# The end of the attention stage: the maximum over partitions behind the first head's power, the last outputs scaled in three parts, the first tile's chain ahead of the second's

## The chip, the core and the metric

The kernel runs on one NeuronCore of a Trainium2 chip. A core has TensorE (PE), VectorE (DVE), ScalarE (ACT), GpSimd (POOL) and SyncE (SP), which here issues nearly all transfers; each runs its own instruction stream and waits for the others on semaphores. The metric is the time of one execution on the device, in microseconds (us), lower is better.

## The reference

A pre-norm decoder layer with three parts over `x` of 16 batches, 256 positions, 512 channels:

```python
x = x + _L0_attn_ref(_layernorm(x, axis=-1), L0_attn_w_qkv, L0_attn_w_proj)
x = x + _L0_xattn_ref(_layernorm(x, axis=-1), L0_xattn_k, fside_S2_0, ctx_2048, ctx_2048, 8)
x = x + _L0_ffn_ref(_layernorm(x, axis=-1), L0_ffn_gate_w, L0_ffn_up_w, L0_ffn_down_w, ...)

def _bitlinear(x, w):        # attention's two linear layers
    xq = round_and_clip(x * 127 / max|x| over the row) / that factor
    wq = round_and_clip(w / mean|w|, -1, 1) * mean|w|
    return xq @ wq.T
# attention: 16 heads of 32 channels, causal softmax, then _bitlinear with w_proj
# mixer: kv = v (x) x2 of each pair of 8 channels, long convolution with k, + kv * skip, times x1, summed
# feed-forward: silu(x @ fp8(gate_w) * gate_scale) * (x @ fp8(up_w) * up_scale), @ fp8(down_w) * down_scale
```

(The lines of `_bitlinear` and the comments are condensed.) The place of the change is the seam between the first part, whose last batch must be scaled, rounded, multiplied and added to `x`, and the second, whose heads need rows of every batch.

## The kernel before

Every engine's stream is written out by hand as a Python function that walks the same step counter, so the order on an engine is the order of the code.

**Attention** goes through `B * PAIRS` = 128 pairs of heads (16 batches, 8 pairs each), one new pair per step. For pair n: `row_max` and `take_max` find the rows' maxima (bank `s_qk`); `probabilities` (PE) writes the scores into bank `s_kq`; `exponentials` (ACT) makes `pT`; `high_part` copies it to `pH` (f16; ACT, the first pair of a batch DVE); `low_part` (POOL) makes the rest `pL`; `weigh` (PE) multiplies both with the values into bank `pv`; `weighed` (ACT) copies `pv` into `oraw`. There is one `s_kq` and one `pv`: the scores of pair n wait for the exponentials of n-1, and `weigh` for the copy before it.

**A batch's end.** `oraw` has for each of two position tiles t and each head 32 outputs in two halves (high and low part of v) and the denominator. The halves are added (tile 0 DVE, tile 1 POOL, `sum_parts`), divided by the denominator (L1063 for the last batch), their largest magnitude is taken (L1066), ACT makes the step of it (L1486), DVE the inverse (L1070, L1074), ACT rounds (L1488), PE turns the tile (`turn_oq`), ACT copies it as `oqT` (L1475), PE multiplies with the weights (`project_out`, L684) and DVE adds the product to `x` (`add_out`, L1045). For the last batch, 15, `finish_last` does this once all 128 pairs are through; batch 14's last steps are mixed in.

**The next part.** SP brings rows of batches 14 and 15 from `x_sb` into `x_grp` as soon as tile 0 of the batch has been added. Head 0 is then prepared (`prepare(0, k)`): DVE takes the moments (L1182 to L1187), POOL raises to the power -1/2 (L1845) and multiplies (L1847), ACT normalises (`v_sb`, L1608), PE turns, ACT copies (`vT`, L1623), and `kv` = `vT` times `cT` in four blocks of 1024 columns: blocks 0 and 1 on DVE (L1194), blocks 2 and 3 on POOL (L1866). `mix` on PE (L803) goes through rows 0, 2, 1, 3 of blocks, two halves each; row 0 needs block 0, row 2 needs blocks 0, 1 and 2. A matmul of f32 shows as two records.

**The maximum over partitions.** The feed-forward part needs a bound of its weights' sizes. `mx` is ready at 425.4 us; POOL's `partition_all_reduce` (L1837) takes the maximum over partitions into `mall`, and DVE makes the scales of it in seven small instructions (`fuse_bound`, L1288 to L1301).
Of the kernel before, what the change touches and what calls it, by code (L numbers as in the profile page):

```python
# [14 lines left out]
P = 128  # L15
# [52 lines left out]
def decoder_kernel(nc, x, skip, ctx_in, w_qkv, w_proj, k_turned, w_gate, w_up, w_down,  # L68
# [21 lines left out]
    HIGH_ON_ACT = (1, 2, 3, 4, 5, 6, 7)  # L90

    with ExitStack() as ctx:
# [164 lines left out]
        high_act, high_dve, low_done = signal("p_high_act"), signal("p_high_dve"), signal("p_low")  # L257
# [36 lines left out]
        PREFETCH_AT, PREFETCHED_AT = B * PAIRS - 2, B * PAIRS + PROB  # L294
# [54 lines left out]
        WEIGHT_BOUND_AT, REDUCE_AT = (PIECES - 1) * PAIRS + CLAMP_AT + 1, (B - 1) * PAIRS + FINISH + 1  # L349
# [6 lines left out]

        def high_done(n):
            b, p = divmod(n, PAIRS)
            if p in HIGH_ON_ACT:
                return high_act, b * len(HIGH_ON_ACT) + HIGH_ON_ACT.index(p) + 1  # L360
            other = [i for i in range(PAIRS) if i not in HIGH_ON_ACT]
            return high_dve, b * len(other) + other.index(p) + 1
# [109 lines left out]
        SCALE_DOWN_AT = 20  # L472
# [73 lines left out]
        def tensor_program(tensor):  # L546
# [83 lines left out]
            def probabilities(n):  # L630
# [4 lines left out]
                def scores(to, h, key, query, first):  # L635
                    r, g = h % R, h // R
                    T.matmul(to, pack[:, 1, r, g, key * P:(key + 1) * P], pack[:, 0, r, g, query * P:(query + 1) * P],  # L637
                             start=first, stop=False)

                w.wait_ge(exp_done, n)  # L640
                T.matmul(s_kq[:, 0:4, :], ident_b[:], mask_kq[:], start=True, stop=False)
                w.wait_ge(mT_low, use + 1)
                for hh in range(2):
                    h = 2 * p + hh
                    for tile in range(2):
                        scores(s_kq[:, 2 * hh + tile, :], h, tile, tile, False)
                    T.matmul(s_kq[:, 2 * hh:2 * hh + 2, :], pick[:, h % H_HEADS, :], nt[:, 0:N], start=False, stop=hh == 1)
                for hh in range(2):
                    h = 2 * p + hh
                    scores(s_kq[:, 4 + hh, :], h, 0, 1, hh == 0)  # L650
                    made = T.matmul(s_kq[:, 4 + hh, :], pick[:, h % H_HEADS, :], nt[:, P:N], start=False, stop=hh == 1)  # L651
                made.then_inc(st_pe, 1)

            def weigh(n):
# [4 lines left out]
                w.wait_ge(low_done, n + 1)  # L659
# [51 lines left out]
            for t in STEPS:  # L711
# [6 lines left out]
                for b, k in batches(t, FINISH, 14):  # L718
# [10 lines left out]
                    elif k == 0:  # L729
                        turn_oq(b, 0)  # L730
# [22 lines left out]
                if t == PREFETCHED_AT:  # L753
                    turn_c(0, misc1)
# [134 lines left out]
        def vector_program(vector):  # L889
# [122 lines left out]

            def finish(b, k):
# [34 lines left out]
            def finish_last():  # L1048
# [9 lines left out]
                w.wait_ge(oqT_pe, 2 * b)
                w.wait_ge(ostep_done, b - 1)
                for t in range(NT):  # L1060
                    if t == 1:
                        w.wait_ge(o_sum, B)
                    V.tensor_tensor(o_sb[:, t, 0:C].rearrange("p (h d) -> p h d", d=D), raw[:, t, :, 0:D],  # L1063
                                    rl[:, t, :].unsqueeze(2).broadcast_to([P, HEADS, D]), ALU.mult).then_inc(o_mult, 1)
                    w.wait_ge(o_mult, b + t + 1)
                    V.tensor_reduce(out=am[:, t:t + 1], in_=o_sb[:, t, :], op=ALU.max, axis=AXIS.X,  # L1066
# [1141 lines left out]
```

## Time and profile before

| | us |
|---|---|
| three timed runs | 1482.04, 1484.29, 1485.83 (median 1484.29) |
| profiled execution | 1481.37 |
| its span, first to last instruction | 1479.6 |
| attention, to the last pair's `oraw` | 0 to 462.2 |
| seam, to the first `mix` matmul | 462.2 to 481.6 |
| mixer and feed-forward | 481.6 to 1479.6 |

PE is busy for 1391.8 us (94%), DVE 1233.3 (83%), POOL 1178.9 (80%), ACT 871.6 (59%). These shares are means over parts with different limits; for a change in the seam only the chain of waits there and what follows on PE count.

### The profile page before, as it was taken

How to read it: one execution, taken by the hardware profiler on the slowest of the kernel's cores; microseconds unless marked ns; L12 is line 12 of the kernel's file. 1: busy time of each engine (PE TensorE's matmuls, PEld its weight loads, DVE VectorE, ACT ScalarE, POOL GpSimd, SP SyncE). 2: the span in 40 equal slices, each digit the busy share in tenths (PEclk: the TensorE clock that was granted, in tenths of full speed). 3: DMA queues.
4: the chain of work that ended last, by engine and by line, in shares of the span. 5: the costliest groups of instructions: out<-in, count | busy, mean ns of one | idle time of the engine just before them, and what ended most of it. 6: DMA issues, size and time to landing. Idle time of an engine off the chain costs nothing.

```text
span 1479.6 us, 23950 instructions
## 1 busy us (share of the span) xinstructions
PE 1391.8 (94%) x8405; PEld 773.0 (52%) x8405; DVE 1233.3 (83%) x1964; ACT 871.6 (59%) x1437; POOL 1178.9 (80%) x902
## 2 busy tenths in 40 slices
PE   3788999999986997999999999999999999999998
PEld 2677878787863442334444444444444444444443
DVE  6889999999884898899898899899889889888511
ACT  5689999999885123544455545464455446544341
POOL 3389999999985787888888888878887888888532
PEclk9899999999997999999999999999999999999999
DMA  5654646464622533222513421432323232240001
GB/s 193 155 126 117 171 133 172 136 171 122 158 67 75 173 79 88 55 57 64 107 44 72 89 61 43 93 78 50 79 65 77 62 76 57 65 100 15 21 15 29
DMA packets 171587, 133.57 MB, mean 90 GB/s; under 512 B 120500, under 2 KB 124748, under 8 KB 171468
## 3 DMA queue, kind: packets, MB, share of 16 engines
q1 hardware_dynamic: 171276, 131.91, 35.6%
q8 instruction: 67, 1.10, 0.3%
q14 instruction: 52, 0.43, 0.1%
q10 hardware_dynamic: 192, 0.14, 0.1%
HBM read 50.67 MB, written 19.92 MB: 48 GB/s over the span
## 4 chain that ended last, share of the span: by engine, by line
PE 65%; DVE 11%; POOL 8%; issue 7%; ACT 6%; DMA 1%; SPq 0%; POOLq 0%; DVEq 0%; ACTq 0%
PE gu L844 20%; PE gu L858 11%; PE shared_bank L789 9%; POOL pL L1796 3%; PE y L811 3%; PE y L808 3%; PE y L805 3%; PE y L813 3%; PE y L814 3%; DVE blockmax L987 2%; DVE o_sb L1027 2%; PE gu L803 1%; PE y L803 1%; DVE qkt L967 1%; ACT pH L1439 1%
## 5 line engine op out<-in xcount | busy, mean ns | idle before, releaser
L1668 ACT ACTIVATE shared<-shared_bank 128x512 f32<-128x512 f32 x162 | 96.2, 594 | 322.9 <-PE shared_bank L789 322.9
L1219 DVE TENSOR_TENSOR y<-shared,y 128x512 f32<-128x512 f32 x324 | 224.1, 692 | 42.7 <-ACT shared L1668 23.0
L1796 POOL TENSOR_TENSOR pL<-pT,pH 128x768 f16<-128x768 f32 x128 | 216.8, 1696 | 13.6 <-ACT pH L1439 7.7
L1226 DVE TENSOR_REDUCE oT<-z 128x64 f32<-128x512 f32 x256 | 175.6, 686 | 8.7
L844 PE MATMUL gu<-fT,wg 128*128 128x512 f16 x768 | 181.4, 379 | 1.5 <-DMA fT<-fnl 1.5
L844 PE MATMUL gu<-fT,wu 128*128 128x512 f16 x768 | 182.5, 381 | 0.0
L1222 DVE TENSOR_TENSOR z<-y,cT 128x512 f32<-128x512 f32 x236 | 162.4, 688 | 11.0 <-PE y L803 4.4
L1930 POOL TENSOR_TENSOR fuL<-fu,fuH 128x512 f16<-128x512 f32 x96 | 112.0, 1166 | 71.7 <-ACT fuH L1683 71.5
L858 PE MATMUL gu<-wd,fuH 128*128 128x512 f16 x384 | 145.5, 379 | 0.0
L858 PE MATMUL gu<-wd,fuL 128*128 128x512 f16 x384 | 145.5, 379 | 0.0
L1866 POOL TENSOR_TENSOR kv<-vT,cT 128x1024 f32<-128x1024 f32 x70 | 137.8, 1970 | 6.1 <-ACT vT L1623 6.1
L844 PEld LDWEIGHTS gu<-fT,wg 128*128 128x128 f16 x768 | 75.0, 98 | 120.5 <-issue 47.4
L844 PEld LDWEIGHTS gu<-fT,wu 128*128 128x128 f16 x768 | 75.5, 98 | 119.5 <-issue 47.2
L1433 ACT ACTIVATE pT<-s_kq,ws 128x768 f32<-128x768 f32 x128 | 115.0, 898 | 26.9 <-PE s_kq L651 20.2
L987 DVE TENSOR_REDUCE blockmax<-s_qk 128x6 f32<-128x768 f32 x124 | 117.6, 948 | 3.9 <-PE s_qk L621 2.7
L789 PE MATMUL shared_bank<-kv_sum,toep 128*128 128x512 f32 x216 | 111.2, 597 | 0.3 <-POOL kv_sum L1854 0.3
L1854 POOL TENSOR_TENSOR kv_sum<-kv 128x1024 f32<-128x1024 f32 x27 | 63.7, 2360 | 55.2 <-DVE kv L1194 55.2
L637 PE MATMUL s_kq<-pack 128*128 128x128 f16 x768 | 99.4, 220 | 0.0
L1241 DVE SCALAR_TENSOR_TENSOR fu<-gu,cols,sil 128x512 f32<-128x512 f32 x96 | 71.4, 743 | 33.6 <-PE gu L844 33.6
L1789 POOL TENSOR_TENSOR qkhl<-qkt,qkhl 128x512 f16<-128x512 f32 x62 | 83.9, 1354 | 19.2 <-ACT qkhl L1419 19.2
L1439 ACT ACTIVATE pH<-pT 128x768 f16<-128x768 f32 x112 | 94.0, 840 | 0.0
L1194 DVE TENSOR_TENSOR kv<-vT,cT 128x1024 f32<-128x1024 f32 x58 | 75.1, 1297 | 14.2 <-ACT vT L1631 11.5
(231 smaller groups left out, 3561.8 us busy)
## 6 DMA issues: line engine op xcount, KB each, us to landing
pack<-qkhl SPq DMA_DIRECT2D x256, 128.0 KB, 2.6
x_sb<-in_x SPq DMA_DIRECT2D x16, 512.0 KB, 4.0
c_sb<-in_ctx SPq DMA_DIRECT2D x32, 256.0 KB, 4.0
hankel<-in_L_xattn_k SPq DMA_DIRECT2D x32, 256.0 KB, 4.1
out_y<-yo SPq DMA_DIRECT2D x32, 256.0 KB, 2.9
x_grp<-x_scratch SPq DMA_DIRECT2D x30, 256.0 KB, 3.5
x_scratch<-x_sb SPq DMA_DIRECT2D x14, 512.0 KB, 3.0
wraw<-in_L_attn_w_qkv SPq DMA_DIRECT2D x3, 1024.0 KB, 9.6
```

Of the source, the lines that this page charges most:

```text
L789: T.matmul(shared_bank[:], tap(h, (2, 0, 1)[part]), (kv_sum, kv12, kv_sum)[part][:, half * HB:(half + 1) * HB, :, :].rearrange("p b j i -> ...
L844: made = T.matmul(bank[:], (wg, wu)[which][:, cb, ib * P:(ib + 1) * P], fT[:, cb, part, :], start=cb == 0 and part == 0, stop=cb == CB - 1 ...
L858: made = T.matmul(bank[:], src[:, t * P:(t + 1) * P], wd[:, ib, :], start=ib == 0 and part == 0, stop=ib == IB - 1 and part == 1)
L987: V.tensor_reduce(out=blockmax[b % 2][:, p, :], in_=score_tile(n)[:, 0:6, :], op=ALU.max, axis=AXIS.X, negate=True).then_inc(max_done, 1)
L1219: chain.step(V.tensor_tensor(bank[:], shared[2 * part + half][:], bank[:], op))
L1222: V.tensor_tensor(z[:], y, weight, ALU.mult).then_inc(m_zm, 1)
L1226: V.tensor_reduce(out=oT[h % 2][:, lb, own].rearrange("p (b j) -> p b j", b=HB), in_=z[:], op=ALU.add, axis=AXIS.X).then_inc(m_z, 1)
L1433: S.activation(pT[n % NP][:], s_kq[:, 0:6, :], ACT.Exp, scale=ws[:, 4:5]).then_inc(exp_done, 1)
L1439: S.activation(pH[n % NP][:], pT[n % NP][:], ACT.Copy).then_inc(high_act, 1)
L1796: G.tensor_tensor(pL[n % 2][:], pT[n % NP][:], pH[n % NP][:], ALU.subtract).then_inc(low_done, 1)
L1866: G.tensor_tensor(block(h, lb), vT[:, lb, :].rearrange("p (b i) -> p b i", b=B).unsqueeze(2).broadcast_to([P, B, M_POS, M_POS]), cT[h % 2] ...
L1930: G.tensor_tensor(fuL[ib][:], fu[n % 2][:], fuH[:, ib, :], ALU.subtract).then_inc(f_fl, 1)
```

## The change

It does six things, all at attention's end.

1. The scores of odd pairs of the last batch go into `s_qk`, which is free once all maxima are taken, so that two score banks take turns.
2. The last pair's `pH` and `pL` are made by DVE (`low_part` on DVE), no longer by ACT and POOL.
3. `toep` and `cT` of head 0 (two ACT copies), and the turning of `c_sb` on PE ahead of `cT`, move from step 136 into the last batch's finish: `toep` between tile 0's rounding and its `oqT` copy, `cT` behind that copy.
4. Tile 0 of the last batch is scaled in three parts, after pairs 4, 7 and 8 of the batch; the first part's halves are added by POOL (`sum_first`). The result lies in `xn`. The maxima of the parts are joined by one more instruction. The step is made by DVE, not ACT.
5. ACT's order becomes tile 0 to its `oqT` copy, then tile 1. On DVE `add_out(14, 0)` moves behind tile 1's scaling.
6. The all-reduce moves on POOL behind the power and product of head 0, in front of its `kv` blocks; `fuse_bound` moves on DVE from the preparation of head 0 to step 8 of the mixer.

The order on POOL, at the change of part, before:

```order
L1796 TENSOR_TENSOR pL1<-pT1,pH1 128x768 [waits pv_pe,p_high_act]
L1801 TENSOR_TENSOR oraw1<-oraw1 128x16x32 [waits pv_out]
L1837 ISA
L1837 ISA mall<-mx 128x4 [waits mx]
L1845 ISA
L1845 TENSOR_TENSOR mstat0<-mstat0,minus_half 128x1 [waits packed2,packed0,v_pe,s_pe,qk_low,st_pe,qk_scaled,m_var,cbc_pe,xqT_pe]
L1847 TENSOR_TENSOR mstat0<-mstat0 128x1 [waits m_rstd]
L1866 TENSOR_TENSOR kv0<-vT,cT0 128x1024 [waits m_vT,m_cT]
```

and on the same engine at the same place after the change:

```order
L1844 TENSOR_TENSOR oraw1<-oraw1 128x8x32 [waits pv_out]
L1849 TENSOR_TENSOR oraw1<-oraw1 128x16x32 [waits pv_out]
L1892 TENSOR_TENSOR mstat0<-mstat0,minus_half 128x1 [waits packed2,packed0,v_pe,s_pe,qk_low,st_pe,qk_scaled,m_var,cbc_pe,xqT_pe]
L1894 TENSOR_TENSOR mstat0<-mstat0 128x1 [waits m_rstd]
L1897 ISA
L1897 ISA mall<-mx 128x4 [waits mx]
L1916 ISA
L1916 TENSOR_TENSOR kv0<-vT,cT0 128x1024 [waits m_vT,m_cT]
```

The last pair's `pL` is gone, half of tile 0's sum is new, and the all-reduce with its two switches stands between the product and `kv` block 2 in place of between the sum and the power.

DVE in the last batch's finish, before:

```order
L1055 RECIPROCAL osmall1<-oraw1 128x32 [waits pv_out]
L1056 TENSOR_TENSOR oraw1<-oraw1 128x16x32
L1063 TENSOR_TENSOR o_sb<-oraw1,osmall1 128x512 [waits oqT_pe,vec_step]
L1066 TENSOR_REDUCE osmall1<-o_sb 128x1 [waits o_mult]
L1070 RECIPROCAL osmall1<-osmall1 128x1 [waits ostep]
L1045 SCALAR_TENSOR_TENSOR x_sb6<-misc2,osmall0,x_sb6 128x512 [waits proj_pe,c2]
L1063 TENSOR_TENSOR o_sb<-oraw1,osmall1 128x512 [waits o_sum]
L1066 TENSOR_REDUCE osmall1<-o_sb 128x1 [waits o_mult]
L1074 RECIPROCAL osmall1<-osmall1 128x1 [waits ostep]
```

and after, from tile 0's third part on:

```order
L1093 RECIPROCAL osmall1<-oraw1 128x2 [waits pv_out]
L1097 TENSOR_TENSOR oraw1<-oraw1 128x2x32
L1081 TENSOR_TENSOR xn<-oraw1,osmall1 128x64 [waits vec_step]
L1107 TENSOR_REDUCE osmall1<-xn 128x1 [waits o_mult]
L1110 TENSOR_SCALAR osmall1<-osmall1 128x1 [waits vec_step]
L1086 TENSOR_SCALAR osmall1<-osmall1 128x1 [waits vec_step]
L1088 RECIPROCAL osmall1<-osmall1 128x1 [waits ostep]
L1112 RECIPROCAL osmall1<-oraw1 128x16
L1081 TENSOR_TENSOR xn<-oraw1,osmall1 128x512 [waits o_sum,vec_step]
L1117 TENSOR_REDUCE osmall1<-xn 128x1 [waits o_mult]
L1086 TENSOR_SCALAR osmall1<-osmall1 128x1 [waits vec_step]
L1088 RECIPROCAL osmall1<-osmall1 128x1 [waits ostep]
```

Behind the last of these rows stands now `add_out(14, 0)`, which stood between the tiles (`x_sb6<-misc2`); behind the last pair only 64 columns of tile 0 are left.

The diff, cut to its core:

```diff
@@ numbers of the plan
-    HIGH_ON_ACT = (1, 2, 3, 4, 5, 6, 7)
+    HIGH_ON_ACT, LAST_HIGH_ON_ACT = (1, 2, 3, 4, 5, 6, 7), (1, 2, 3, 4, 5, 6)
+        LAST_AT = B * PAIRS - 1 + LOW
+        LAST_PARTS = ((0, PAIRS // 2), (PAIRS // 2, PAIRS - 1), (PAIRS - 1, PAIRS))
+        LOW_ON_DVE = [B * PAIRS - 1]
+        def scores_tile(n):
+            return s_qk if n > (B - 1) * PAIRS and n % 2 == 1 else s_kq
@@ PE, probabilities
-                w.wait_ge(exp_done, n)
+                if n > (B - 1) * PAIRS:
+                    w.wait_ge(exp_done, n - 1)
+                    w.wait_ge(max_done, B * PAIRS)
+                else:
+                    w.wait_ge(exp_done, n)
+                to = scores_tile(n)
@@ PE, the last batch
                     elif k == 0:
+                        turn_c(0, misc1)
                         turn_oq(b, 0)
                         project_out(b, 0)
                         project_out(b - 1, 1)
@@ DVE, finish_last
+                for i, (begin, stop) in enumerate(LAST_PARTS):
+                    first, end = 2 * begin, 2 * stop
+                    w.wait_ge(pv_out, PAIRS * b + stop)
+                    chain.step(V.reciprocal(rl[:, 0, first:end], raw[:, 0, first:end, D]))
+                    if i == 0:
+                        w.wait_ge(o_sum, B)
+                    else:
+                        chain.step(V.tensor_tensor(raw[:, 0, first:end, 0:D], raw[:, 0, first:end, 0:D], raw[:, 0, first:end, VW:VW + D], ALU.add))
...
+                step_last(0)
+                chain.step(V.reciprocal(rl[:, 1, :], raw[:, 1, :, D]))
                 chain.wait()
...
+                w.wait_ge(o_sum, B + 1)
+                scale_heads(1, 0, HEADS).then_inc(o_mult, 1)
...
+                step_last(1)
+                w.wait_ge(c2_done, b)
+                add_out(b - 1, 0)
                 w.wait_ge(c2_done, b + 1)
                 add_out(b, 0)
                 add_out(b - 1, 1)
@@ DVE, mixer
-                if k == 1:
-                    fuse_bound()
+                if g == FUSE_BOUND_AT:
+                    fuse_bound()
@@ ACT, finish_last
                 for t in range(NT):
-                    w.wait_ge(omax_done, b + t + 1)
-                    S.activation(step[:, t:t + 1], am[:, t:t + 1], ACT.Copy, scale=1.0 / 127.0).then_inc(ostep_done, 1)
                     w.wait_ge(oscale_done, b + t + 1)
-                    S.activation(o_sb[:, t, 0:C], o_sb[:, t, 0:C], ACT.Copy, bias=ROUND, scale=inv[:, t:t + 1]).then_inc(o_round, 1)
+                    S.activation(xn[:, t, 0:C], xn[:, t, 0:C], ACT.Copy, bias=ROUND, scale=inv[:, t:t + 1]).then_inc(o_round, 1)
...
+                        projected(w)
+                        turn_taps(0)
+                    copy_oqT(b, t)
+                    if t == 0:
+                        copy_cT(0, misc1)
@@ POOL
+            def sum_first():
+                raw, heads = oraw[(B - 1) % 2], slice(0, 2 * LAST_PARTS[0][1])
...
-                if t == REDUCE_AT:
-                    w.wait_ge(mx_done, 1)
-                    G.partition_all_reduce(mall[:], mx[:], P, RMAX).then_inc(mall_done, 1)
@@ POOL, prepare
                     G.tensor_tensor(shift, shift, rstd, ALU.mult).then_inc(m_shift, 1)
+                    if h == 0:
+                        w.wait_ge(mx_done, 1)
+                        G.partition_all_reduce(mall[:], mx[:], P, RMAX).then_inc(mall_done, 1)
```

## Rows read from the trace of the kernel before

**Rows 1.** Chain of waits through the seam: start us, us, what.

```profile
461.85 0.40 ACT oraw L1447
...
468.97 0.59 ACT oqT L1475
...
469.69 1.88 PE misc L684 x4
...
472.44 1.96 DMA x_grp<-x_sb
...
475.76 0.71 issue
...
481.58 3.75 PE y L803 x4
```

**Rows 2.** ACT in order of time: start us, us, instruction [idle before <-releaser].

```profile
456.37 0.62 ACT L1505 ACTIVATE toep<-hankel 128x512 f32<-128x512 f32 x1
...
457.48 0.38 ACT L1447 ACTIVATE oraw<-pv 128x260 f32<-128x260 f32 x1
457.75 0.84 ACT L1439 ACTIVATE pH<-pT 128x768 f16<-128x768 f32 x1
...
465.92 0.72 ACT L1488 ACTIVATE o_sb<-o_sb,osmall 128x512 f32<-128x512 f32 x1 [0.23 <-DVE osmall L1070]
```

**Rows 3.** DVE in order of time, through the seam and head 1.

```profile
438.59 0.55 DVE L1011 CAST pH<-pT 128x768 f16<-128x768 f32 x1
...
464.69 0.69 DVE L1066 TENSOR_REDUCE osmall<-o_sb 128x1 f32<-128x513 f32 x1
...
476.48 0.18 DVE L1288 TENSOR_TENSOR bound<-mall 128x2 f32<-128x2 f32 x1
...
477.66 0.23 DVE L1301 TENSOR_SCALAR cols<-cols,bound 128x12 f32<-128x12 f32 x1
...
502.69 0.69 DVE L1222 TENSOR_TENSOR z<-y,cT 128x512 f32<-128x512 f32 x1 [2.02 <-PE y L803]
...
505.02 0.14 DVE L1187 TENSOR_SCALAR mstat<-mstat 128x1 f32<-128x1 f32 x1
```

**Rows 4.** POOL in order of time, from the last pair to head 2's power.

```profile
458.68 1.64 POOL L1796 TENSOR_TENSOR pL<-pT,pH 128x768 f16<-128x768 f32 x1 [0.58 <-ACT pH L1439]
462.31 1.06 POOL L1801 TENSOR_TENSOR oraw<-oraw 128x512 f32<-128x512 f32 x1 [2.00 <-ACT oraw L1447]
469.17 0.39 POOL L1837 PARTITION_ALL_REDUCE mall<-mx  x1 [5.79 <-issue]
476.47 0.59 POOL L1845 TENSOR_TENSOR mstat<-mstat,minus_half 128x1 f32<-128x1 f32 x1 [6.92 <-DVE mstat L1187]
...
480.25 2.99 POOL L1866 TENSOR_TENSOR kv<-vT,cT 128x1024 f32<-128x1024 f32 x1 [2.92 <-ACT vT L1623]
...
486.34 1.95 POOL L1866 TENSOR_TENSOR kv<-vT,cT 128x1024 f32<-128x1024 f32 x1
...
505.25 0.75 POOL L1845 TENSOR_TENSOR mstat<-mstat,minus_half 128x1 f32<-128x1 f32 x1 [2.75 <-DVE mstat L1187]
```

**Rows 5.** By line: POOL's library switches, xcount, duration ns, first and last start us.

```profile
L1742 POOLq MODIFY_POOL_CONFIG  x2: 11/11/11, 1.3 to 1.4; - x2
...
L1837 POOLq MODIFY_POOL_CONFIG  x2: 11/11/11, 463.3 to 463.4; - x2
...
L1845 POOLq MODIFY_POOL_CONFIG  x2: 82/82/83, 469.5 to 469.5; - x2
```

**Rows 6.** Windows: us, busy of PE, PEld, DVE, ACT, POOL; PEclk; DMA share; GB/s.

```profile
449.70:453.00 3.30, 3.10 (x35) 2.39 (x31) 2.46 (x1) 2.33 (x4) 3.30 (x3) 0.50 0.00 0
...
466.80:473.50 6.70, 4.82 (x15) 2.29 (x16) 2.15 (x5) 1.62 (x5) 0.39 (x1) 0.50 0.03 5
...
481.60:487.10 5.50, 5.50 (x7) 2.40 (x8) 5.29 (x8) 0.70 (x2) 3.10 (x4) 0.50 1.03 337
487.30:502.40 15.10, 15.10 (x42) 7.05 (x41) 9.14 (x15) 2.14 (x3) 11.67 (x8) 1.00 0.59 175
```

More of the change, by code:

```diff
@@ L355, in decoder_kernel, with high_on_act, low_parted @@
         wq8 = wq8_dram.rearrange("m n p c -> m (n p c)").rearrange("m (n p c) -> m n p c", p=P, c=PIECE)
+        def high_on_act(n):
+            return n % PAIRS in (HIGH_ON_ACT if n < (B - 1) * PAIRS else LAST_HIGH_ON_ACT)
         def high_done(n):
[L358 to L362, printed above, removed]
+            by_act = high_on_act(n)
+            return high_act if by_act else high_dve, sum(high_on_act(m) == by_act for m in range(n + 1))
+        def low_parted(n):
+            if n in LOW_ON_DVE:
+                return low_last, LOW_ON_DVE.index(n) + 1
+            return low_done, n + 1 - sum(m < n for m in LOW_ON_DVE)
+        def scores_tile(n):
+            return s_qk if n > (B - 1) * PAIRS and n % 2 == 1 else s_kq
         W_ORDER = (1, 0, 2, 3)
@@ L471, in row_of @@
             return SHARED_ROWS[s // 2]
-        SCALE_DOWN_AT = 20
+        FUSE_BOUND_AT, SCALE_DOWN_AT = 8, 20
         def groups(g, begin, steps):
@@ L1053, in finish_last @@
                 rl = osmall[:, 4 * NT:4 * NT + NT * HEADS].rearrange("p (t h) -> p t h", t=NT)
-                w.wait_ge(pv_out, PAIRS * B)
-                chain.step(V.reciprocal(rl, raw[:, :, :, D]))
-                chain.step(V.tensor_tensor(raw[:, 0, :, 0:D], raw[:, 0, :, 0:D], raw[:, 0, :, VW:VW + D], ALU.add))
-                chain.wait()
[L1058 to L1066, printed above, removed]
-                                    apply_absolute_value=True).then_inc(omax_done, 1)
-                    if t == 0:
-                        w.wait_ge(ostep_done, b + 1)
-                        V.reciprocal(inv[:, 0:1], step[:, 0:1]).then_inc(oscale_done, 1)
-                        w.wait_ge(c2_done, b)
-                        add_out(b - 1, 0)
@@ L1073, in finish_last, with scale_heads @@
-                w.wait_ge(ostep_done, b + 2)
-                V.reciprocal(inv[:, 1:2], step[:, 1:2]).then_inc(oscale_done, 1)
+                w.wait_ge(xqT_pe, 2 * B)
+                w.wait_ge(c2_done, b - 1)
+                chain.step(V.tensor_scalar(xn[:, :, C], ones[:, 0:NT], ws[:, 1:2], EPS, ALU.mult, ALU.mult))
+                def scale_heads(t, first, end):
+                    return V.tensor_tensor(xn[:, t, first * D:end * D].rearrange("p (h d) -> p h d", d=D), raw[:, t, first:end, 0:D],
+                                           rl[:, t, first:end].unsqueeze(2).broadcast_to([P, end - first, D]), ALU.mult)
@@ new lines, in finish_last @@
+                step_last(0)
+                chain.step(V.reciprocal(rl[:, 1, :], raw[:, 1, :, D]))
+                chain.wait()
+                w.wait_ge(o_sum, B + 1)
+                scale_heads(1, 0, HEADS).then_inc(o_mult, 1)
+                w.wait_ge(o_mult, b + 2)
+                chain.step(V.tensor_reduce(out=am[:, 1:2], in_=xn[:, 1, :], op=ALU.max, axis=AXIS.X, apply_absolute_value=True))
+                step_last(1)
+                w.wait_ge(c2_done, b)
+                add_out(b - 1, 0)
@@ L1141, in vector_program @@
                         low_max(use)
-                if (n := pair(t, HIGH)) is not None and n % PAIRS not in HIGH_ON_ACT:
+                if (n := pair(t, LOW)) in LOW_ON_DVE:
+                    low_part(n)
+                if (n := pair(t, HIGH)) is not None and not high_on_act(n):
                     high_part(n)
@@ L1552, in scalar_program @@
                     copy_weights(i, blocks)
-                if (n := pair(t, HIGH)) is not None and n % PAIRS in HIGH_ON_ACT:
+                if (n := pair(t, HIGH)) is not None and high_on_act(n):
                     high_part(n)
@@ L1820, in gpsimd_program @@
             for t in STEPS:
-                if (n := pair(t, LOW)) is not None:
+                if (n := pair(t, LOW)) is not None and n not in LOW_ON_DVE:
                     low_part(n)
+                if t == LAST_AT:
+                    sum_first()
                 for b, k in batches(t, FINISH, 1):
```

70 lines of the change are left out of this document (42 added, 28 removed).

## The prediction

> **What bounds the kernel now.** I read the chain of waits first, then each engine in order of time through the seam, then windows around it. The chain shows that from the last `oraw` copy (461.85) to the first `mix` matmul (481.58) one thing waits for another: 19.7 us in which no engine is full [rows 1]. From 481.58 on PE runs without a pause: 5.50 busy of 5.50, then 15.10 of 15.10 [rows 6]. So a microsecond taken out of the seam moves the whole mixer forward, unless PE runs into something that did not move with it. The reader is to see two other things. After the all-reduce POOL is not simply free [rows 4, 5]. And the granted clock after a pause of PE is 0.50 (1.2 GHz) for a while, 1.00 (2.4 GHz) again later [rows 6].
>
> **The change part by part.** All times are on the axis of the profiled execution (1481.37 us, span 1479.6, so 1.8 lie around it); it is 2.9 under the median of the runs, 1484.29.
>
> *The last `oraw` (parts 1 to 3).* In ACT's queue `toep` and `cT` stand from 456.37 to 457.48, 1.11 us, and behind them the copy that `weigh` of the next pair waits for; the last pair's `pH` costs up to 0.84 more there [rows 2]. POOL's last `pL` runs from 458.68 to 460.32 [rows 4]; on DVE the trace shows no such subtraction. Its bound from below is the 0.55 of the cast of 768 columns, from above POOL's 1.64 [rows 3, 4]; I take 0.96, since 512 columns cost 0.69 [rows 3], and DVE is idle there. Removing the 1.11 is certain; of the 0.84 a part is met by the turns through `pv` that remain; together I take 1.5 (1.1 to 1.95): the last copy starts at 460.35 in place of 461.85. The second score bank saves nothing by itself, since the exponentials there wait for POOL's `pL`, which the bank doesn't touch.
>
> *Tile 0 in three parts (4).* Before, the rounding starts at 465.92, 3.67 after the last copy's end (462.25) [rows 1, 2]. After the change seven small instructions follow the last copy; six starts of such take 1.18, from 476.48 to 477.66 [rows 3], so about 1.4. But DVE comes to them late: `pL` of the last pair until 458.8, then part one (two instructions of 256 columns, 0.42 each by the same line through 512 columns and the small ones) and part two (three of 192, 0.36 each), with gaps and reciprocals to 461.5. So the rounding starts at 463.1, 2.8 earlier.
>
> *Order of the tiles (5).* Before, tile 0's `oqT` copy (468.97) stands behind tile 1's rounding on ACT, 2.3 after the end of its own (466.64), and the multiplication starts at 469.69 [rows 1, 2]. After the change PE turns at 463.8 and ACT copies at 465.0. What is late next is `add_out(14, 0)`: it frees the bank that `project_out(15, 0)` takes, and now stands behind tile 1's whole chain on DVE: 0.25, 0.69, 0.69 [rows 3], two small ones, then 0.75, which end at 465.85. So the multiplication starts at 465.95: 3.7 earlier. The DMA of the rows (issued at 472.44, 1.96 us) [rows 1] and the moments shift by the same.
>
> *POOL's power.* In head 2 it starts 0.09 after DVE's release (505.16 to 505.25); in the seam the chain has 0.71 of issue between the release (475.76) and the power (476.47) [rows 1, 3, 4]. With the all-reduce no longer ahead some 0.7 go. The product then ends at 472.9 in place of 477.33, and `vT`, `kv` block 0 and the first `mix` matmul follow 4.4 earlier: 477.1 in place of 481.58.
>
> *The all-reduce's new place (6).* From the end of POOL's sum (463.37) to the start of the power (476.47) the all-reduce holds, or may hold, 13.1 us: 5.80 from the switch (463.4) to the all-reduce, 0.39 for it, and 6.91 from its end (469.56) to the power [rows 4, 5]. The first two are certain. Of the last 6.91 the wait for DVE covers 6.20; that the power came 0.7 later than it should says that POOL wasn't ready when DVE was. I read it as code loaded after a switch: 5.8 one way and up to 6.9 back. Its bounds are 0.7 (only a slow first call) and 6.91. I take 6.91, since the first switch took nearly as long without any wait, and since a shorter load back would have let the power start at the release. The switches at 1.3 cost nothing visible [rows 5], which speaks for the lower end; but there the standard code may have been in place already.
>
> Now this hides behind tile 1's chain and the DMA. After the change it stands in front of `kv` block 2: 472.9 + 13.1 = 486.0, and with 1.95 for the block [rows 4] it is ready at 487.95. PE needs it for the third product of row 2, after eight records. At the low clock these take 6.9 us (the seventh was under way when 5.50 were over) [rows 6]: PE stands from 484.0 to 488.0. Before, it reached the same product at about 487.8, the eighth record going at the high clock, with the block ready at 483.24 [rows 4, 6]. So the whole 4.4 us go back in one wait, and 0.2 more.
>
> The Trainium skill (GPSIMD Engine Reference, Instruction dispatch) says that the first call to a freshly loaded kernel pays about 6 us of code loading, 5.95 measured after MODIFY_POOL_CONFIG, with no instruction shown. This trace agrees for the all-reduce, 5.79 [rows 4]. For the way back, with the page's figure in place of 6.91, the block would be ready 1.0 earlier; read as paid by the call itself, whenever it comes, it would have put the power at 481.7, which the trace excludes.
>
> *The clock.* Before, PE is at 1.00 from 487.1 on. After a wait of 4 us it should come back low, as after its other pauses: low for 3.3 us from 449.7 and for 6.7 us from 466.8 [rows 6]. Half of that is lost, 1.65 to 3.35; I take 2.2 (0 if the pause is not noticed).
>
> *`fuse_bound`.* Seven instructions, 1.4 us from 476.48 to 477.9 [rows 3], free today because DVE waits there. Step 8 puts them into head 1 behind the 2.02 us in which DVE waits for PE [rows 3], so they don't fill that gap; there the banks ahead of PE may or may not take them up. 0 to 1.4, I take 0.6. The later `kv` blocks, `kv_skip` and head 1's power on POOL start 2 to 3 us later against PE, within gaps that POOL has in heads 0 and 1 (it is busy for 11.67 of 15.10) [rows 6]: nothing.
>
> Sum: -4.4 + 4.6 + 2.2 + 0.6 = +3.0 on the profiled execution, and the same on the median: 1487.3, rounded to 1487.
>
> **The rivals.**
> *A. Return without a load.* POOL is free 0.7 after the all-reduce. Then block 2 is ready at 472.9 + 5.8 + 0.4 + 0.7 + 1.95 = 481.8, before PE wants it at 484.0. For it: the free switches at the program's start; against it: the late power. Time: 1484.3 - 4.4 + 0.6 = 1480.5 (1478.5 to 1482.5).
> *B. The loads get slower: a loss.* Until 473.5 the DMA share was 0.03; from 481.6 it is 1.03 at 337 GB/s [rows 6], since SP then brings the feed-forward weights. The loads now fall into that. If code comes through the same memory and the 12.7 us become longer by a third to a half, PE waits another 4 to 6 us: 1491 to 1494, at 1492. It decides from a stretch of 12% on, where the total passes the bound below. For it: transfers there take longer; against it: no queue in the profile carries these loads.
> *C. The chain isn't shortened.* DVE's three parts collide with POOL's sum, or the last copy moves less: 2 us of the 4.4 are missing, block 2 comes later by as much: 1489.5.
>
> **How the numbers follow.** A run of this kernel can tell about 0.3%, 4.45 us, from no change: faster is under 1479.8, slower over 1488.7. Forecast (POOL held, PE waits): 0.62, of which 0.50 within the bound, 0.11 slower, 0.01 faster. A: 0.20, with 0.08 faster, 0.12 within. B: 0.12, slower 0.11. C: 0.06, slower 0.03. That gives faster 0.09, same 0.66, slower 0.25. The forecast's own range is 1484 to 1490.5. The range of all reaches down into A and up to the edge of B: 1480 to 1491.5; it leaves out the third of A with the largest gain and most of B, less than 2 in 10.
>
> **What would show it.** Right: the first `mix` matmul 4 to 5 us earlier against the last `oraw` of before (about 477), the power 0.1 after DVE's release, MODIFY_POOL_CONFIG right behind head 0's product, the all-reduce 5.8 later, `kv` block 2 about 13 us after the product, and PE idle for about 4 us in row 2 with POOL's `kv` as releaser, then a low clock. A is right if block 2 starts within 7.5 us of the product and PE shows no wait. B is right if the all-reduce starts over 7 us after its switch. I am wrong in the first part if `project_out(15, 0)` does not start near 466, and in the size if the clock stays at 1.00 after the wait.

## The result, and the profile after

The changed kernel takes **1490.0 us** (median of 5 runs, 1487.8 to 1492.2), the kernel before 1485.8 beside it (5 runs, 1482.0 to 1486.1): the ratio is 1.0035, 95% interval 1.0023 to 1.0048. The forecast was 1487.0. The profiled execution of after has a span of 1488.4 us, 8.8 more than that of before. Of these, 2.0 lie ahead of everything that the change touches: on POOL, `pL` starts at 419.07 us where it started at 417.08, and at 438.65 instead of 436.66, both ahead of the first pair whose scores are in another bank. Times of after in the seam are therefore compared with before's plus 2.0.

POOL of after in order of time (start us, us, instruction [idle before <-releaser]), beside [rows 4]:

```profile
475.88 0.56 POOL L1892 TENSOR_TENSOR mstat<-mstat,minus_half 128x1 f32<-128x1 f32 x1 [11.30 <-DVE mstat L1235]
476.52 0.19 POOL L1894 TENSOR_TENSOR mstat<-mstat 128x1 f32<-128x1 f32 x1
483.74 0.39 POOL L1897 PARTITION_ALL_REDUCE mall<-mx  x1 [7.03 <-issue]
491.62 1.94 POOL L1916 TENSOR_TENSOR kv<-vT,cT 128x1024 f32<-128x1024 f32 x1 [7.49 <-issue]
```

The library switches of after, by line (xcount, ns, first and last start us), beside [rows 5]:

```profile
L1897 POOLq MODIFY_POOL_CONFIG  x2: 11/11/11, 476.7 to 476.7; - x2
```
```profile
L1916 POOLq MODIFY_POOL_CONFIG  x2: 83/83/83, 484.1 to 484.1; - x2
```

PE of after in order of time, where row 2 stands still:

```profile
480.50 3.75 PE L820 MATMUL y<-kv,toep 128*128 128x512 f32 x4 [2.11 <-DVE kv L1242]
484.04 3.20 PE L820 MATMUL gu<-kv,toep 128*128 128x512 f32 x4
493.62 2.07 PE L820 MATMUL gu<-kv,toep 128*128 128x512 f32 x2 [6.38 <-POOL kv L1916]
```

Windows of after: us, busy of PE, PEld, DVE, ACT, POOL; PEclk (the clock granted to TensorE, 0.50 being 1.2 GHz); DMA share; GB/s, beside [rows 6]:

```profile
487.30:493.60 6.30, 0.00 (x0) 0.00 (x0) 0.00 (x0) 0.00 (x0) 1.98 (x2) 0.72 0.37 105
493.60:497.20 3.60, 3.58 (x8) 2.05 (x9) 1.44 (x3) 1.41 (x2) 3.39 (x4) 0.54 0.02 5
497.20:512.00 14.80, 14.80 (x39) 6.72 (x38) 9.36 (x14) 2.17 (x3) 10.03 (x7) 1.00 0.65 170
```

The reader is to see a core in which nothing computes for 4 us. The switch stands right behind POOL's multiplication with head 0's power (L1894); from 476.71 to 491.62, **14.9 us**, POOL executes one instruction of 0.39. Block 2 of `kv` waited for nothing else: its `vT` was there at 479.03. PE has done the two products that it can, waits 6.38 us for the block, and comes back at 1.2 GHz for 3.6 us. The front of the seam did get shorter: the first `mix` matmul starts at 480.50, against 481.58 + 2.0 [rows 1], 3.1 earlier. The third product of row 2, the first that needs block 2, starts at 493.62 against 487.88 + 2.0, 3.7 later, and head 1's products at 509.95 instead of 502.49, 5.5 later after the same correction.

### The profile page after: what moved, and what is told of

The parts are those of the page before. It is cut to its first block, busy times and chain, and to the rows that moved or that the text cites. A ratio compares the mean times of both kernels' runs of the same rounds, so it can differ in the third digit from the quotient of the medians.

```text
span 1488.4 us, 23963 instructions
## 1 busy us (share of the span) xinstructions
PE 1394.3 (94%) x8405; PEld 774.1 (52%) x8405; DVE 1235.1 (83%) x1978; ACT 870.5 (58%) x1434; POOL 1178.2 (79%) x902
## 4 chain that ended last, share of the span: by engine, by line
PE 63%; DVE 12%; POOL 8%; issue 8%; ACT 6%; DMA 2%; SPq 1%; POOLq 0%; DVEq 0%; ACTq 0%
PE gu L861 20%; PE gu L875 10%; PE shared_bank L806 9%; PE y L830 3%; PE y L831 3%; PE y L822 3%; PE y L825 3%; PE y L828 3%; POOL pL L1839 3%; DVE blockmax L1004 2%; DVE o_sb L1049 2%; DVE z L1270 1%; PE misc L702 1%; DVE qkt L984 1%; DVE osmall L1055 1%
## 5 line engine op out<-in xcount | busy, mean ns | idle before, releaser
L1839 POOL TENSOR_TENSOR pL<-pT,pH 128x768 f16<-128x768 f32 x127 | 215.7, 1701 | 15.4 <-PE pv L687 6.3
L1481 ACT ACTIVATE pT<-s_kq,ws 128x768 f32<-128x768 f32 x124 | 111.3, 898 | 26.4 <-PE s_kq L669 19.8
L1242 DVE TENSOR_TENSOR kv<-vT,cT 128x1024 f32<-128x1024 f32 x58 | 73.2, 1263 | 15.8 <-ACT vT L1674 12.7
```

The costliest lines, as they stand in the source:

```text
L1481: S.activation(pT[n % NP][:], scores_tile(n)[:, 0:6, :], ACT.Exp, scale=ws[:, 4:5]).then_inc(exp_done, 1)
L1839: G.tensor_tensor(pL[n % 2][:], pT[n % NP][:], pH[n % NP][:], ALU.subtract).then_inc(low_done, 1)
```

## The experiments

The times of before ran on the same chip as each experiment; ratios are to it.

**1. The all-reduce moved, alone.** Before, with part 6 of the change only:

```diff
-                if t == REDUCE_AT:
-                    w.wait_ge(mx_done, 1)
-                    G.partition_all_reduce(mall[:], mx[:], P, RMAX).then_inc(mall_done, 1)
...
                     G.tensor_tensor(shift, shift, rstd, ALU.mult).then_inc(m_shift, 1)
+                    if h == 0:
+                        w.wait_ge(mx_done, 1)
+                        G.partition_all_reduce(mall[:], mx[:], P, RMAX).then_inc(mall_done, 1)
```

> The kernel before with the sixth edit alone: the all-reduce behind head 0's product on POOL, fuse_bound at step 8. Theory (code loads hold POOL ahead of kv block 2, and PE waits there): the product ends some 0.7 us earlier, block 2 is ready about 17 us behind it, PE waits 5 to 6 us in row 2 and comes back at the low clock; together 6 to 9 us slower than before. Rival (the loss of the changed kernel comes from the rearranged finish, parts 1 to 5, and the all-reduce is harmless): within 1.5 us of before.

Measured: 1494.64 us, ratio **1.0069** (1.0050 to 1.0087). PE of this run:

```profile
480.52 3.75 PE L803 MATMUL y<-kv,toep 128*128 128x512 f32 x4 [2.11 <-DVE kv L1194]
484.06 1.98 PE L803 MATMUL gu<-kv,toep 128*128 128x512 f32 x4
492.86 2.07 PE L803 MATMUL gu<-kv,toep 128*128 128x512 f32 x2 [6.82 <-POOL kv L1866]
```

The loss is in this part, and it is larger without the rest of the change. It is also larger than was expected: 10.2 us by the ratio, where 6 to 9 stood, with a wait of PE of 6.82 where 5 to 6 stood; the way back took 7.85 here.

**2. Everything but that.** After, with the all-reduce and `fuse_bound` at their old places.

> The changed kernel with the sixth edit undone: all-reduce behind the last sum on POOL, fuse_bound in head 0's preparation. Theory (the way back to the standard code costs about 7 us whenever POOL has nothing to wait for, and now shows since the power is wanted earlier): the power starts 13 to 13.5 us after the sum's end and not when DVE releases it; 1 to 2 us faster than before. Rival (the way back is free and the 0.7 us were a slow first call): the power starts under 1 us after DVE's release, 2.5 to 3 us faster than before.

Measured: 1482.19 us, ratio **0.9989** (0.9980 to 0.9999). POOL of this run in order of time:

```profile
463.46 1.10 POOL L1849 TENSOR_TENSOR oraw<-oraw 128x512 f32<-128x512 f32 x1 [2.42 <-ACT oraw L1495]
470.82 0.39 POOL L1887 PARTITION_ALL_REDUCE mall<-mx  x1 [6.26 <-issue]
478.69 0.59 POOL L1895 TENSOR_TENSOR mstat<-mstat,minus_half 128x1 f32<-128x1 f32 x1 [7.47 <-issue]
```

DVE had released the power at 475.29 (its last small instruction: 475.15 and 0.14 long). The power starts 3.4 us after that, with no wait on record: the way back is bare here, 7.5 us from the all-reduce's end. Before, it was covered by the wait for DVE [rows 4]. So the place behind the last sum had just enough room for the old finish, and it holds up the new one; that is what the change ran away from, to a place with less room.

**3 and 4. No maximum over partitions.** After and before without the all-reduce: the bound is made from each partition's own maxima, so this step of the computation is missing in both.

```diff
-                w.wait_ge(mall_done, 1)
-                chain.step(V.tensor_tensor(bound[:], mall[:, 0:2], mall[:, 2:4], ALU.mult))
+                w.wait_ge(mx_done, 1)
+                chain.step(V.tensor_tensor(bound[:], mx[:, 0:2], mx[:, 2:4], ALU.mult))
...
-                        G.partition_all_reduce(mall[:], mx[:], P, RMAX).then_inc(mall_done, 1)
```

> The changed kernel without the all-reduce; the bound is taken from each partition's own maxima, so the maximum over partitions is left out. Theory: no wait of PE in row 2, high clock through it; 8 us faster than the changed kernel, about 3 to 4 us faster than before (0.2 to 0.3%). Rival (the finish costs as much as it gains): not faster than before.

> The kernel before without the all-reduce (bound from each partition's own maxima). Theory: the power starts 0.1 us after DVE's release, everything else as before: 0.7 us faster, no more. Rival (the all-reduce costs more there than the 0.7 us seen): over 1.5 us faster.

Measured: after without it 1479.84, ratio **0.9971** (0.9960 to 0.9982); before without it 1483.26, ratio **0.9998** (0.9989 to 1.0008). POOL and PE of the first of the two:

```profile
479.04 2.99 POOL L1913 TENSOR_TENSOR kv<-vT,cT 128x1024 f32<-128x1024 f32 x1 [2.46 <-ACT vT L1666]
```
```profile
480.37 3.36 PE L820 MATMUL y<-kv,toep 128*128 128x512 f32 x4 [2.11 <-DVE kv L1242]
483.56 2.74 PE L820 MATMUL gu<-kv,toep 128*128 128x512 f32 x6
```

One instruction of 0.39 us and its two switches cost nothing that can be measured in before's place on before's finish, 0.18% on the new finish in the old place (the two intervals just touch), and 0.64% (9.5 us) on the new finish in the new place. In the trace of before without it the power starts 0.17 us after the end of DVE's last small instruction (477.27 to 477.44), in before 0.79 after it (475.68 to 476.47): the expected 0.7 is there, too small for the times. The rearranged finish by itself gains 0.3%.

**5. The maximum on TensorE.** Since a transfer of the operation to another engine needs no switch, the same maximum is made there. Nothing is left out: four matmuls put the 128 partial maxima into one row of every partition, and DVE reduces them in the finish.

```diff
                         turn_c(0, misc1)
+                        w.wait_ge(exp_done, B * PAIRS)
+                        w.wait_ge(mx_done, 1)
+                        for j in range(4):
+                            made = T.matmul(s_kq[:, j, :], mx[:, j:j + 1].broadcast_to([P, P]), ident[:], start=True, stop=True)
+                        made.then_inc(mx_pe, 1)
...
                 add_out(b - 1, 0)
+                w.wait_ge(mx_pe, 1)
+                V.tensor_reduce(out=mall[:], in_=s_kq[:, 0:4, :], op=ALU.max, axis=AXIS.X).then_inc(mall_done, 1)
```

PE waits for `mall_done` before the mixer reuses the bank; `fuse_bound` is back at its old place.

> The changed kernel with the maximum over partitions taken off GpSimd: in TensorE's idle time behind the turned mixing taps (about 464.8 to 467.8 us) four matmuls of the column of mx, broadcast to 128 columns, by the identity put all 128 partition maxima into a row of every partition, and VectorE reduces 4x128 of them to mall behind its first add in the finish (idle there from 469.6 to 471.7 us). The bound is computed at its old place. Theory (the code load there and back is the whole loss): no MODIFY_POOL_CONFIG record at the seam, block 2 follows block 0's power within about 4 us, TensorE's third product of row 2 starts without a wait, time as with the maximum left out, 1479.8 us beside 1483.5 (ratio 0.997, within 0.001). Rival (the maximum's extra work costs where it is put): four matmuls of f32 with a stationary operand of stride zero are slow or VectorE's 0.7 us stands on the path to the last outputs, the first mix starts 0.5 to 1 us later and the ratio is 0.998 or more.

Measured: 1479.14 us, ratio **0.9969** (0.9958 to 0.9980): faster than before, and by the two ratios 0.66% faster than the change. Its rows on PE, on DVE and on POOL:

```profile
464.89 1.06 PE L752 MATMUL s_kq<-ident,mx 128*128 128x128 f32 x8
```
```profile
469.83 0.68 DVE L1128 TENSOR_REDUCE mall<-s_kq 128x4 f32<-128x512 f32 x1
```
```profile
476.66 0.19 POOL L1902 TENSOR_TENSOR mstat<-mstat 128x1 f32<-128x1 f32 x1
479.77 2.99 POOL L1921 TENSOR_TENSOR kv<-vT,cT 128x1024 f32<-128x1024 f32 x1 [2.91 <-ACT vT L1674]
```

Both engines stood idle there, so 1.06 us of PE and 0.68 of DVE replace 14.9 of POOL. The ratio is that of the run without any maximum. The rival, that the extra work shows, asked for 0.998 or more, which is the end of the interval, and for a first `mix` 0.5 to 1 us later. Counted from the last `oraw` copy the first `mix` is 0.3 later than in run 3 (17.8 against 17.5); the turn of `v_sb` takes 1.08 here and 0.63 there.

**6. The first add earlier.** As 5, and `add_out(B - 2, 0)` stands ahead of tile 1's chain instead of behind it.

```diff
                 step_last(0)
+                w.wait_ge(c2_done, b)
+                add_out(b - 1, 0)
                 chain.step(V.reciprocal(rl[:, 1, :], raw[:, 1, :, D]))
...
                 step_last(1)
-                w.wait_ge(c2_done, b)
-                add_out(b - 1, 0)
```

> As the run with the maximum on TensorE, and VectorE's add of the next to last batch's first tile (0.75 us, 468.88 in the changed kernel) stands ahead of tile 1's chain and not behind it. Theory (the projection of the last batch's tile 0, 469.69 us, is held by this add and not by the turned outputs, whose copy ends at 469.16): the projection starts 0.5 us earlier (within 0.2), when the copy ends, and with it the last outputs, the power and the first mix; tile 1's rounding starts 0.8 us later and holds nothing. Time 0.4 us less than the run it is compared with, not measurable by itself. Rival: the next projection (14,1) and the turn of tile 1 wait for the rounding, and nothing is gained.

Measured: 1480.67 us, ratio 0.9979 (0.9968 to 0.9990), not to be told from run 5. In the trace the releaser changes:

```profile
468.79 3.09 PE L702 MATMUL misc<-wprojT,oqT 128*128 128x512 bf16 x8 [0.78 <-ACT oqT L1531]
```

The projection starts 0.75 after the start of the `oqT` copy (468.04), where it was 1.13 in run 5 (468.84 to 469.97): 0.4 us, as expected. In after the same matmul names DVE's add (`[1.17 <-DVE x_sb L1067]`, below).

**7. GpSimd's sum held back.** As 6, and GpSimd sums tile 1 only when DVE's sum for part two is done.

```diff
                 w.wait_ge(pv_out, PAIRS * (b + 1))
+                if b == B - 1:
+                    w.wait_ge(second_summed, 1)
```

> As the run before it, and GpSimd's sum of tile 1's halves (1.07 us at 463.51) waits until VectorE's sum for part two is done. In the changed kernel that VectorE sum took 1.08 us beside GpSimd's and 0.32 in the run with parts one to five alone, where GpSimd's sum came at the same moment by only 0.05 us less. Theory (the two engines hold each other up when both sum at once): VectorE's sum takes 0.3 to 0.4 us, GpSimd's starts some 0.4 us later and ends before tile 1's chain asks for it, rounding of tile 0 starts 0.6 to 0.7 us earlier against the pv copy before it. Rival (the 1.08 us is a wait for ScalarE's last copy of pv or the like, that stands in the record as duration): it stays over 0.9 us.

Measured: 1479.41 us, ratio 0.9966 (0.9956 to 0.9977). In after (first fence) and in this run (second), all engines in order of time:

```profile
463.04 0.39 ACT L1495 ACTIVATE oraw<-pv 128x260 f32<-128x260 f32 x1
...
463.51 1.07 POOL L1849 TENSOR_TENSOR oraw<-oraw 128x512 f32<-128x512 f32 x1 [0.92 <-ACT oraw L1495]
...
463.71 1.08 DVE L1097 TENSOR_TENSOR oraw<-oraw 128x192 f32<-128x192 f32 x1
...
467.09 0.72 ACT L1534 ACTIVATE xn<-xn,osmall 128x512 f32<-128x512 f32 x1 [2.98 <-DVE osmall L1088]
...
469.69 3.54 PE L702 MATMUL misc<-wprojT,oqT 128*128 128x512 bf16 x8 [1.17 <-DVE x_sb L1067]
```
```profile
464.09 0.32 DVE L1103 TENSOR_TENSOR oraw<-oraw 128x192 f32<-128x192 f32 x1
...
464.56 1.17 POOL L1864 TENSOR_TENSOR oraw<-oraw 128x512 f32<-128x512 f32 x1 [2.74 <-DVE oraw L1103]
...
465.18 0.63 DVE L1103 TENSOR_TENSOR oraw<-oraw 128x64 f32<-128x64 f32 x1
```

In after, DVE's sum of 192 columns takes 1.08 us; it ends at 464.79, 0.21 after GpSimd's (464.58). Held apart it takes 0.32. The 64-column sum, which now falls beside GpSimd's, takes 0.63 and ends at 465.81, 0.08 after it (465.73). From the start of the last `oraw` copy to the rounding of tile 0 it is 3.44 us; in after it is 4.05. This looks like a wait until the other engine has finished, and not like a slowdown in proportion. The Trainium skill (SBUF — State Buffer, SBUF: two separate sides) says so: a DVE instruction with two SBUF inputs and a GpSimd instruction that reads SBUF exclude each other for the whole of the instruction that came first. These rows agree, and so do those of run 2: there DVE's sum of 192 columns starts 0.14 ahead of GpSimd's (463.32 and 463.46) and takes 0.32, and the DVE product behind it takes 1.10 instead of 0.36.

**8. The maximum twice.** After, with the all-reduce issued a second time behind the first.

> The changed kernel with the all-reduce issued twice in a row. Theory (the 7 us ahead of the all-reduce and the 7.5 behind it are code loads, one for each change of library): one pair of MODIFY_POOL_CONFIG there and one back, the second all-reduce follows the first within about 0.3 us and takes 0.4, kv block 2 comes 0.5 to 0.7 us later than with one, time 0.7 us above the changed kernel's (about 1488.7 beside 1483.5 on such a chip). Rival (each call of such a function costs its 7 us by itself): 7 us more ahead of block 2, 1495 or above.

Measured: 1490.49 us, ratio **1.0041** (1.0025 to 1.0057). POOL in order of time:

```profile
486.45 0.39 POOL L1897 PARTITION_ALL_REDUCE mall<-mx  x1 [7.22 <-issue]
486.94 0.37 POOL L1899 PARTITION_ALL_REDUCE mall<-mx  x1
494.25 1.94 POOL L1918 TENSOR_TENSOR kv<-vT,cT 128x1024 f32<-128x1024 f32 x1 [6.94 <-issue]
```

The second call costs 0.49 us, all in all. The 7 us ahead and the 7 behind belong to the change of library and not to the call. That they are code being loaded remains a reading: no DMA queue of the profile carries such a transfer in these stretches.

**9. The weight loads held.** After, and the SP queue waits for block 2 before it loads gate, up and down weights.

```diff
+                if g == 0:
+                    w.wait_ge(*kv_made(0, 2))
                 if g < 2 * CB:
                     gate_up_load(g)
```

> The changed kernel, and the sync engine waits for kv block 2 of head 0 before it issues the loads of gate and up weights (8 of 384 KB) and of the first down weights, which ran from 478.8 us on beside the code loads (DMA share 0.8 to 1.06 between 477 and 488 us; 0.12 in the 5.8 us ahead of the all-reduce in the kernel before). Theory A (the code load is fetched beside the data and stretched by it): from the first MODIFY_POOL_CONFIG record to the all-reduce 5.8 to 6.3 us instead of 7.0, the way back 7.0 or less instead of 7.5, block 2 comes 1 to 1.7 us earlier relative to the power. Theory B (the times differ for another reason, such as what was loaded before): 7.0 and 7.5 stay within 0.2. The whole time may rise, since the weights come some 12 us later; it decides nothing.

Measured: 1490.69 us, ratio 1.0045 (1.0030 to 1.0060). POOL in order of time, and the windows (us, busy of POOL, PEclk, DMA share, GB/s):

```profile
483.82 0.39 POOL L1897 PARTITION_ALL_REDUCE mall<-mx  x1 [7.51 <-issue]
491.45 1.94 POOL L1916 TENSOR_TENSOR kv<-vT,cT 128x1024 f32<-128x1024 f32 x1 [7.25 <-issue]
```
```profile
480.00:484.00 4.00, 0.18 (x1) 0.50 0.35 113
484.00:488.00 4.00, 0.21 (x1) 0.73 0.00 0
488.00:492.00 4.00, 0.55 (x1) 0.70 0.00 0
```

The way back takes 7.25 us with no DMA traffic at all (7.49 in after with a share of 1.06 in its first half): theory A, that the weights stretch the loads, has fallen there. For the way there the run decides less, since context and taps still load in its first part. It took 7.51 at a mean share of 0.52, in after 7.03 at 0.82, and in run 1, at the same place, 6.31 at 0.81; before, the share was 0.12 and the time 5.80. So the length does not follow the traffic, and why the way there took 5.80 before [rows 4], 6.26 in run 2 and 6.3 to 7.5 at the new place stays open. Theory B expected 7.0 and 7.5 within 0.2; the 7.51 and 7.25 differ from them by 0.5 and 0.25, so the length can differ by that much at one and the same place.

**10. Held for both sums.** As 7, until DVE's sum for part three is done.

> As the run with GpSimd's sum of tile 1 held back, but held until VectorE's sum for part three is done as well. In that run the 192-column sum had fallen from 1.08 to 0.32 us, and the 64-column sum, now beside GpSimd's, had risen from 0.20 to 0.63. Theory (they hold each other up whenever both run): both are at 0.32 and 0.20 us, tile 0 is rounded 3.0 us after the start of the last copy of pv (3.44 with part two alone held, 4.06 without), GpSimd's sum takes 1.07 or less again. It ends by about 466.2 us, and VectorE asks for it at 467.9, so nothing else moves. Rival (the 64-column sum is long for another reason): it stays at 0.6. The time is 0.4 us less at best, which these rounds can't tell.

Measured: 1476.87 us, ratio **0.9953** (0.9936 to 0.9969). All engines in order of time:

```profile
460.58 0.39 ACT L1508 ACTIVATE oraw<-pv 128x260 f32<-128x260 f32 x1 [1.17 <-PE pv L687]
...
460.87 0.32 DVE L1103 TENSOR_TENSOR oraw<-oraw 128x192 f32<-128x192 f32 x1
...
461.96 0.21 DVE L1103 TENSOR_TENSOR oraw<-oraw 128x64 f32<-128x64 f32 x1
...
462.31 1.06 POOL L1864 TENSOR_TENSOR oraw<-oraw 128x512 f32<-128x512 f32 x1 [3.71 <-DVE oraw L1103]
...
463.49 0.72 ACT L1547 ACTIVATE xn<-xn,osmall 128x512 f32<-128x512 f32 x1 [1.41 <-DVE osmall L1094]
```

All three sums have their undisturbed length, and the rounding comes 2.91 us after the last copy's start, 1.14 earlier than in after. Of these, 0.76 are the sum for part two (1.08 to 0.32), which is the hold's doing. The other 0.38 are the constant column (L1078 in after, 0.59; 0.22 here), which is not: run 8 holds nothing, and there it takes 0.21. This is the fastest kernel of the study. Its interval overlaps those of runs 5 and 7, so the gain over them is seen in the trace only: from the last copy to the first `mix` matmul 15.4 us here, 17.8 in run 5, 17.5 in after, 19.7 before [rows 1]. Of the 2.4 against run 5, 1.2 lie ahead of the rounding, 0.4 between it and the projection (run 6's edit), and 0.8 behind the projection's start, whose eight matmuls take 1.89 here and 3.45 there.

## Why the prediction came out as it did

The forecast was +3.0 us, +2.4 of it by the start of head 1's products. The trace has +5.5 there, and the medians +4.2 (by the ratio +5.2). The mechanism is the one of the forecast: POOL held by the two switches, PE waiting in row 2 for block 2, a low clock behind the wait. Its sizes were off: what comes ahead of the switches shrank by less than forecast and the loads took longer, 1.8 us each and both to the same side, against 0.5 from the clock and 0.6 from `fuse_bound` to the other. That 1490.0 still lies within the forecast's own range, by 0.5, is owed to the range's width and in part to luck.

- **The last `oraw`: 1.5 earlier forecast, 0.8 measured** (463.04 against 461.85 + 2.0). `pL` of the last pair on DVE takes 1.25 us, not 0.96: POOL's `pL` runs until 461.28, and DVE's needs 0.94 when alone (run 10). POOL's own `pL` there takes 2.08 instead of 1.64 beside DVE's cast of the last pair (0.54); in run 2 it is the other way round, 1.64 for POOL and 1.93 for the cast:

```profile
459.20 2.08 POOL L1839 TENSOR_TENSOR pL<-pT,pH 128x768 f16<-128x768 f32 x1 [0.96 <-PE pv L687]
...
460.85 1.25 DVE L1033 TENSOR_TENSOR pL<-pT,pH 128x768 f16<-128x768 f32 x1
...
461.25 1.34 POOL L1844 TENSOR_TENSOR oraw<-oraw 128x256 f32<-128x256 f32 x1
...
462.02 0.59 DVE L1078 TENSOR_SCALAR xn<-ones,ws 128x2 f32<-128x2 f32 x1
```

- **The rounding of tile 0: 2.8 earlier forecast, 0.8 measured.** This is the largest miss. The forecast, too, had the rounding wait for DVE, but had DVE through `pL` at 458.8 and through parts one and two at 461.5; with the 2.0 taken off, the trace has 460.1 and 463.5. DVE was not idle ahead of `pL`, as the forecast had it: an add that waits 0.40 for PE stands there (460.18, 0.75 long), and `pL` starts 1.0 later than forecast. It takes 0.3 more, and the two parts take 3.4 instead of 2.7. What follows takes the 1.6 of the forecast. From 460.18 to 466.97 DVE works without a pause, and three instructions in that stretch are long because POOL is at work: `pL` (1.25, alone 0.94), the constant column, which the sum had left out (0.59, alone 0.21 as in run 2; it ends at 462.61, POOL's sum at 462.59), and the sum for part two (1.08, alone 0.32). Together that is 1.45 us; in run 10, where none of the three is long, it takes 1.43 less from the start of `pL` to the rounding (4.81 against 6.24). The forecast named this as a rival (C, "DVE's three parts collide with POOL's sum") at 0.06; it happened, beside the forecast's own mechanism and not in its place. That rival's price, 1489.5, lies nearest to the measured time.
- **The projection: 3.7 earlier forecast, 2.0 measured.** The gate was named rightly: `[1.17 <-DVE x_sb L1067]`, the add behind tile 1's chain. Run 6 sizes it at 0.4 us.
- **The power: 0.7 forecast, 0.6 measured.** It starts 0.18 after the end of DVE's last small instruction (475.70 to 475.88), in before 0.79 (475.68 to 476.47).
- **The two code loads: 13.1 us forecast, 14.9 measured.** The choice of the upper bound for the way back was right (run 2: 7.5 bare; 7.49 in after), and 0.6 short of the truth, as 6.91 was only what could be seen of it. The way there took 7.03 instead of 5.80. Rival A, a return without a load, is refuted by runs 1, 2 and 8. Rival B's threshold, 12% on 12.7 us, was passed (7.03 and 7.49 are 14% more), and so was its sign, an all-reduce over 7 us after its switch (7.03), but the time stayed under its 1491. Its reason, the traffic, is not borne out: run 9 has 7.25 for the way back without any, and run 1 has 6.31 for the way there at a share of 0.81.
- **PE's wait.** Forecast: the wait gives back the whole shift of 4.4 and 0.2 more, so that the product that needs block 2 starts 0.2 later than before. Measured: 3.7 later. The miss is the 1.8 of what comes ahead of the switch (POOL's multiplication ends at 476.71, forecast 472.9 + 2.0) and the 1.8 of the loads.
- **The clock: 2.2 forecast, 1.7 measured.** 3.58 us of PE work at 0.54 after the wait; at 1.00 they would have taken 1.9. From 493.62 to head 1 the kernel loses 5.46 - 3.74 = 1.7.
- **`fuse_bound`: 0.6 forecast, none measured.** In after its seven instructions run in head 1 from 513.34 to 515.68, 2.34 us, since the last of them falls beside a `kv` block on POOL (1.19 instead of 0.23). DVE gets later by that, but PE doesn't wait: it is 7.46 us later than before at the start of head 1 (502.49 and 509.95) and still 7.46 later in the next head. The times agree: at step 8 (run 3) the ratio is 0.9971, at its old place (run 5) 0.9969. In after:

```profile
514.49 1.19 DVE L1349 TENSOR_SCALAR cols<-cols,bound 128x12 f32<-128x12 f32 x1
546.04 1.88 PE L820 MATMUL y<-kv,toep 128*128 128x512 f32 x4
```

  and in before:

```profile
538.58 1.88 PE L803 MATMUL y<-kv,toep 128*128 128x512 f32 x4
```

The two misses of 1.8 and the clock's -0.5 turn the forecast's +2.4 at head 1 into the +5.5 of the trace. Of the rest of the 8.8 us of span, 2.0 lay ahead of the seam and 1.3 came up behind 546 us; where these 1.3 come from is not settled.

## What to carry to other kernels

Count a GpSimd instruction from another library by its two switches, not by itself: 14.1 to 15.1 us of the engine in these runs for an instruction of 0.39, of which a wait can hide all or nothing. Look for the idle stretch that holds both ways, or make the result on engines that stand idle: four small matmuls and a reduction did it in 1.7 us. Where VectorE and GpSimd work in the same microseconds, add up their instructions as if they excluded each other, and make the one that isn't urgent wait by a semaphore: that brought one sum from 1.08 to 0.32 us here with no other work moved. It holds for some VectorE instructions only: in these traces sums and products of two tensors in SBUF, a cast and operations with a scalar were long beside GpSimd. A product with one input from TensorE's bank and a reduction were not. In before they take 0.69 each, as elsewhere, beside the `kv` block that POOL makes from 486.34 to 488.29 [rows 4]:

```profile
486.81 0.69 DVE L1222 TENSOR_TENSOR z<-y,cT 128x512 f32<-128x512 f32 x1
487.54 0.69 DVE L1226 TENSOR_REDUCE oT<-z 128x64 f32<-128x512 f32 x1
```

## What the runs showed of the hardware

- The way back to the standard library is about as long as the way there: 6.94 to 7.85 us back (7.49 in after, 7.85 in run 1, 7.47 in run 2, 6.94 in run 8, 7.25 in run 9) and 6.26 to 7.51 there in the same runs, 5.80 in before. Before showed only the way there bare, since the way back lay under a wait. That a plain multiplication of two tensors has to wait for it is new against what the trace of before could tell.
- The way back starts at the switch, not when the next instruction is ready: before, the power came 0.7 late after 6.91 us, most of which was a wait for DVE [rows 4].
- TensorE's clock in the projections goes with the pause ahead of them. In after it stands idle for 3.09 us before the turn at 467.87 and then does the eight matmuls at 0.53; in run 7 the matmuls of the maximum end at 467.80, right ahead of the turn at 467.91, and the eight run at 1.00:

```profile
469.69:473.23 3.54, 3.54 (x10) 0.53 0.05 9
```
```profile
469.35:471.25 1.90, 1.90 (x10) 1.00 0.05 10
```

  In run 5 the same matmuls of the maximum end at 465.95, 2.2 us ahead of the turn, and the eight take 3.45 us. Work of one microsecond, put at the end of a pause instead of its start, goes with 1.6 us less here. In run 7 the clock had also been low just before (0.50 from 463.10 to 465.90 us) and had risen again. Run 2 speaks against that as the reason: it had such a low stretch too (0.50 from 463.00 to 465.40), had no matmuls of the maximum, stood idle for 1.34 us ahead of the turn, and its eight took 3.47 us at 0.54. But its projection also came 0.4 us later behind the turn, for want of run 6's edit, and the place of the matmuls was not tried by itself.
